# Two stages of a graph kernel joined into one program: feed-forward layer and second attention

## The reference

```python
# layer 0
attn = softmax(q @ k.T / sqrt(32))                       # 8 heads
out  = sum_r (attn * (adj == r)) @ (x @ Wv[r])           # 4 relations
x    = layernorm(x + out @ Wo + bo)
x    = layernorm(x + gelu(x @ W1 + b1) @ W2 + b2)        # feed-forward, width 1024
# layer 1
e    = leaky_relu(q @ k.T, 0.2)                          # 8 heads of 32
attn = softmax(where(adj > 0, e, -9e15))
h    = layernorm(attn @ v)
out  = layernorm(concat(h, x) @ Wffn.T) + x
```

## Time and profile before

| | before |
|---|---|
| median of 3 runs | 3193.49 us (3193.42 to 3193.79) |
| the profiled execution | 3191.47 us |
| its span, first to last instruction | 3189.7 us |
| mean granted clock of PE | 0.98 of full |
| PE busy | 3005.9 us, 94% |
| DVE, ACT, POOL busy | 2509.3, 1999.1, 1683.6 us |
| feed-forward, first to last matmul | 1207.6 to 1881.1 us |
| second attention, from its first load's issue | 1894.3 us to the end |

### The profile page before, as it was taken

How to read it: one execution, slowest core, us unless ns; L and a number is a source line. 1 busy time by engine, 2 the same in 40 slices (tenths; PEclk the granted TensorE clock), 3 DMA queues, 4 the chain that set the end, 5 groups by cost and what they waited for, 6 DMA issues and landing times. The chain is left out here.

```text
span 3189.7 us, 74979 instructions
## 1 busy us (share of the span) xinstructions
PE 3005.9 (94%) x27720; PEld 2053.4 (64%) x27909; DVE 2509.3 (79%) x6757; ACT 1999.1 (63%) x3695; POOL 1683.6 (53%) x1510
## 2 busy tenths in 40 slices
PE   6999999999999958999999977999999999999996
PEld 4666666666666635666666645777777777777774
DVE  5888888888888855776667646888888888888883
ACT  3666666666665635666666634777777777777774
POOL 2555555554555542444444442666666666666665
PEclk9999999999999989999999989999999999999998
DMA  5444444454545413222222213444444444444441
GB/s 158 139 135 137 137 134 142 132 143 133 145 128 144 128 55 101 74 79 75 72 80 79 68 60 121 144 140 142 143 134 135 146 135 142 145 135 135 146 131 44
DMA packets 358328, 382.45 MB, mean 120 GB/s; under 512 B 99265, under 2 KB 266817, under 8 KB 357953
## 3 DMA queue, kind: packets, MB, share of 16 engines
q1 hardware_dynamic: 356800, 376.03, 39.3%
q10 hardware_dynamic: 1152, 1.52, 0.2%
HBM read 242.16 MB, written 118.49 MB: 113 GB/s over the span
## 5 line engine op out<-in xcount | busy, mean ns | idle before, releaser
L2456 DVE TENSOR_TENSOR f_gl<-f_act,f_gh 128x512 f16<-128x512 f32 x256 | 302.9, 1185 | 205.4 <-ACT f_act L2382 205.3
L1844 ACT ACTIVATE b_prob<-b_score_t 128x512 f32<-128x512 f32 x512 | 304.4, 595 | 246.0 <-PE b_score_t L2107 245.9
L2034 DVE CUSTOM_DVE_ANT_0 b_junk<-b_score,b_mask 128x256 bf16<-128x256 f32 x1024 | 390.3, 418 | 40.6 <-issue 40.3
L1408 DVE TENSOR_TENSOR a_linked<-a_prob,a_mask 128x1024 f32<-128x1024 f32 x256 | 356.9, 1395 | 2.3 <-ACT a_prob L1205 2.2
L1928 POOL TENSOR_TENSOR b_half_sum<-b_prob 128x512 f32<-128x512 f32 x256 | 335.5, 1311 | 42.9 <-ACT b_prob L1844 42.6
L2377 ACT ACTIVATE f_gh<-f_up,s_f_b 128x512 f16<-128x512 f32 x256 | 175.5, 686 | 255.1 <-PE f_up L2506 255.0
L1205 ACT ACTIVATE a_prob<-a_score_t 128x1024 f32<-128x1024 f32 x256 | 259.5, 1014 | 110.8 <-PE a_score_t L1488 104.4
L1916 POOL TENSOR_TENSOR b_nw_root<-b_nw_var,b_minus_halves 128x2 f32<-128x2 f32 x128 | 113.1, 883 | 404.9 <-DVE b_nw_neg_mean L1975 404.9
L1401 DVE TENSOR_REDUCE a_neg_max<-a_score 128x4 f32<-128x1024 f32 x256 | 307.2, 1200 | 4.1 <-PE a_score L1501 4.1
L1850 ACT ACTIVATE b_score_t<-b_score_t 128x512 f32<-128x512 f32 x512 | 305.6, 597 | 0.3 <-PE b_score_t L2116 0.3
L2504 PE MATMUL f_down<-s_w,f_gh 128*128 128x256 f16 x1024 | 279.2, 273 | 1.3 <-DVE f_gl L2456 1.3
(11 more groups left out here) (233 smaller groups left out, 9149.5 us busy)
## 6 DMA issues: line engine op xcount, KB each, us to landing
a_stack<-qk_scratch SPq DMA_DIRECT2D x384, 128.0 KB, 3.0
b_stack<-qk_scratch SPq DMA_DIRECT2D x384, 128.0 KB, 2.8
qk_scratch<-a_qk SPq DMA_DIRECT2D x64, 512.0 KB, 2.9
qk_scratch<-b_qk SPq DMA_DIRECT2D x64, 512.0 KB, 2.8
a_x_sb<-x_t SPq DMA_DIRECT2D x64, 256.0 KB, 3.2
a_adj_sb<-adj_t SPq DMA_DIRECT2D x64, 256.0 KB, 3.3
a_res<-x_nodes SPq DMA_DIRECT2D x64, 256.0 KB, 3.4
after_attention<-a_z_out SPq DMA_DIRECT2D x64, 256.0 KB, 2.5
```

The costliest lines, as they stand in the source:

```text
L1408: nc.vector.tensor_tensor(linked[:, k], prob[:, k], mask[:, be[1] % 2].unsqueeze(1).to_broadcast([P, 2, NT * N]), ALU.mult).then_inc(link_ ...
L1844: nc.scalar.activation(prob[:, he], score_t[s][:].rearrange("p t n -> p (t n)"), ACT.Exp, scale=ALPHA).then_inc(exp_done, 1)
L2034: last = nc.vector.tensor_tensor_reduce(junk[:, s, it], score[s][:, it], mask[:, i, it], -1.0, 3e38, ALU.add, ALU.min, neg_max[:, i, col:c ...
L2456: nc.vector.tensor_tensor(gl[:, bu[1] % 2, f], act32[:, f % 2], gh[:, bu[1] % 2, f], ALU.subtract).then_inc(low_done, 1)
```

## The change

`feed_forward` and `attention_second` no longer have blocks of their own. Each returns, for every engine, a function `slot(t, h)` that issues the instructions of one eighth of a step, and a new function calls the two in turn inside one block:

```diff
+def feed_forward_and_second(nc, mid1, mid2, out, adj, adj_t, scr, scr_m, shared, w, late):
+    JOIN = 31
+    CONSTANTS = JOIN - 6
...
+        banks = {k: ctx.enter_context(nc.psum_tensor("bank_" + k, [P, 512], F32)) for k in (
+            "pair0", "pair1", "heads", "sums", "proj", "back", "score0", "score1")}
+        first_rows = ctx.enter_context(nc.sbuf_tensor("first_rows", [P, 2, 2, HQ, DC * N], F16))
...
+        def run(first_slot, second_slot, constants=None):
+            for n in range(JOIN + second["steps"]):
+                for h in range(H):
+                    if n < first["steps"]:
+                        first_slot((n // U, n % U), h)
+                    if constants and n == CONSTANTS and h == 7:
+                        constants(n)
+                    if n >= JOIN:
+                        second_slot(((n - JOIN) // U, (n - JOIN) % U), h)
```

So step `n` of the whole holds step `n` of the feed-forward (up to 34) and step `n - 31` of the attention. The end of the feed-forward's block, the wait for its last store there, the barrier of its block and the start of the attention's block are gone. For both sets of buffers to fit, some are shared and some made smaller:

```diff
-        down = [psum(f"down{i}", [P, 512]) for i in range(4)]
+        row, up, down = banks["proj"], [banks["pair0"], banks["pair1"]], [banks["heads"], banks["sums"]]
...
-        x_sb = sb("x_sb", [P, 4, TT, D], F32)
-        xb = sb("xb", [P, 4, TT, D], F32)
+        x_sb = sb("x_sb", [P, 2, TT, D], F32)
+        xb = sb("xb", [P, XBS, TT, D], F32)
...
-                        if f % 2 == 0 and (n := after(back(bd, 1), TT, k + 1)) is not None:
-                            pe.wait_ge(y_ready, n)
+                        if f % 2 == 0 and number(bd) * TT + k >= 2:
+                            pe.wait_ge(y_ready, number(bd) * TT + k - 1)
...
-    XS = 4
+    XS = 2
...
-        prob = sb("prob", [P, H, NT * N], F32)
-        half_sum = sb("half_sum", [P, H, N], F32)
+        prob = over("gh", 0, [P, H, NT * N], F32)
+        half_sum = over("xb", 0, [P, H, N], F32)
```

```diff
-            nc.gpsimd.memset(stack[KQ:P, :, 1], SHIFT).then_inc(stack_set, 1)
+            def first_constants(n):
+                pool.wait_ge(finished["roots"][0], 2 * (n - 1))
+                wait_old(pool, "row_out", "split")
+                nc.gpsimd.memset(first_rows[KQ:P, :, 1], SHIFT).then_inc(stack_set, 1)
...
+            def late_constants():
+                wait_old(pool, "down_done", "roots")
+                nc.gpsimd.memset(late_rows[KQ:P, :, 1], SHIFT).then_inc(stack_set, 1)
```

More of the change, by code:

```diff
@@ L1597, in attention_first, with attention_second @@
     nc.all_engine_barrier()
[L1600 removed]
+def attention_second(nc, ctx, x_in, x_out, adj, adj_t, scr, scr_m, ident, late, banks, first_rows, old, finished):
     L = "b_"
@@ L1766, in column, with sync, slot @@
             return (h % HQ) * DC * NT + (h // HQ) * NT + it
-        block = ctx.enter_context(nc.Block())
-        @block.sync
-        def _(sp):
+        def sync(sp):
             def held(value):
                 return value if value is None or isinstance(value, int) else sp.to_reg(value)
-            def step(t):
-                for h in range(H):
+            def slot(t, h):
+                if True:
                     if bx := due(t, h, "load"):
@@ L1918, in root, with slot @@
                 nc.gpsimd.tensor_tensor(shift[k][:], s["neg_mean"][:], s["root"][:], ALU.mult).then_inc(root_chain[k], 1)
-            def step(t):
-                for h in range(H):
+            def slot(t, h):
+                if True:
+                    if number(t) == LATE and h == 0:
+                        late_constants()
                     if half := half_due(t, h, "halved"):
@@ L1950, in step, with vector @@
                         nc.gpsimd.tensor_tensor(z_out[:, i], z_out[:, i], res[:, i], ALU.add).then_inc(affine, 1)
-            run_steps(pool, step, STEPS_TAIL)
-        @block.vector
-        def _(dve):
+            return slot, first_constants
+        def vector(dve):
             nc.vector.memset(minus_halves[:], -0.5)
@@ L2081, in step, with tensor @@
                         norm_stats(bg, 1, y[:, bg[1] % 2], y_ready)
-            run_steps(dve, step, STEPS_TAIL)
-        @block.tensor
-        def _(pe):
+            return slot
+        def tensor(pe):
             def three(out, lhs_h, lhs_l, rhs_h, rhs_l, start, stop):
@@ L2243, in step, with feed_forward @@
                         last.then_inc(sums_turned, 1)
-            run_steps(pe, step, STEPS_TAIL)
-    nc.clear_and_free_semaphores(sems)
-    nc.all_engine_barrier()
-def feed_forward(nc, x_in, x_out, shared, w, late):
+            return slot
+        return {"sync": sync, "scalar": scalar, "gpsimd": gpsimd, "vector": vector, "tensor": tensor, "steps": B + STEPS_TAIL}, sems
+def feed_forward(nc, ctx, x_in, x_out, shared, w, late, banks, first_rows):
     G = 2
@@ L2438, in step, with vector @@
                     nc.gpsimd.tensor_tensor(shift[:], s["neg_mean"][:], s["root"][:], ALU.mult).then_inc(root_chain, 1)
-            run(pool, step)
-        @block.vector
-        def _(dve):
+            return slot
+        def vector(dve):
             nc.vector.memset(minus_halves[:], -0.5).then_inc(prep, 1)
@@ L2450, in _, with slot @@
             nc.vector.tensor_scalar(late["far_ident"][:], ident[:], FAR, None, ALU.mult)
-            def step(t):
+            def slot(t, f):
                 bx, bu, bd, bn = stages(t)
-                for f in range(FC):
+                if True:
                     if have(bu):
@@ L2496, in step, with tensor @@
                     nc.vector.tensor_scalar(s["neg_mean"][:], mv[:, :, 0], -1.0, None, ALU.mult).then_inc(seed_chain, 1)
-            run(dve, step)
-        @block.tensor
-        def _(pe):
+            return slot
+        def tensor(pe):
             def three(out, lhs_h, lhs_l, rhs_h, rhs_l, start, stop):
```

279 lines of the change are left out of this document (170 added, 109 removed).

## The result

| | before | the change |
|---|---|---|
| median of 4 runs | 3193.64 us (3193.42 to 3194.10) | 3156.49 us (3153.71 to 3160.38) |
| ratio | | 0.9878, 95% interval 0.9865 to 0.9890 |
| profiled execution, its span | 3191.47 us, 3189.7 us | 3157.04 us, 3155.3 us |

The change is faster by 37.2 us, 1.2%; 3157.0 us were predicted. The runs of the change scatter more than these four of before (6.7 us against 0.7), and in the later measurements the kernel before scatters as much, from 3185.04 to 3198.25 us. So a step of the argument is read from the traces and not from these medians.

What follows compares the result with a forecast made beforehand. From 1881.08 to 1950.53 a chain bounds the kernel, elsewhere PE's own list. Step 4 of the attention starts at 1914.1 instead of 1950.53, 36.4 us less: 3155.0 profiled, 3157 median; range 3150 to 3167.

Steps and rivals of the forecast that it cites:

- Step 32: Feed-forward step 32 with attention step 1: 20.85 us plus 4.7 of PE work and 0.2 for DVE, ending at 1874.6.
- Step 33: Feed-forward step 33 with attention step 2: 11.4 us plus 6.2 of added work and 0.6 of waiting, ending at 1892.8.
- Scores of graph 1: In attention step 3, PE waits 4.3 us for graph 1's rows through the scratch tensor; scores start at 1897.9.
- Rest of step 3: From graph 1's scores to attention step 4: 15.1 us as before, with matmuls at half clock behind the wait.
- Second memset: POOL's 3.5 us memset near DVE's mask: delays the offset 0 or 2.3 us; half, 1.1 us, taken.
- First memset, banks, places: Step 25's memset, two down banks and fewer or moved buffer places in the feed-forward: 0 cost, 1 us kept for the memset's range.
- Barrier and stores: At the join of the stages: their cost vanishes in what is already counted, since PE no longer waits for them.
- weaving rival: Attention held back until the feed-forward ends: only store, barrier and block start saved, some 13 us; 3180 us; chance 0.04.
- waiting links: In steps 32 to 34, some six links each cost 1.5 to 2 us, 10 us come back: 3167 us; chance 0.12.
- slower loop: Late y with two down banks stops PE every feed-forward step; at 1.5 us a step 3203 us; chance 0.08.
- no weaving: Same as the weaving rival: attention waits for the feed-forward's end, some 13 us saved, 3180 us; chance 0.04.
- the one that keeps the clock up: At graph 1's rows PE waits under 2 us and the clock may hold: 3150 to 3152 us; chance 0.14.

Runs made afterwards that it cites:

- e5: The change measured again, unedited, against the kernel before; 3158.62 us, 0.9891 of before, join 136.2 us.
- e9: e7 plus a tiny unused Exp on ACT behind the moved normalisation, so the table load falls in ACT's idle time; 3156.18 us, join 138.1 us.
- e11: The change plus 40 matmuls of 256 columns, unused by the result, on PE ahead of the scores of graph 1; 3155.54 us, join 133.6 us.
- e8: The change with the second memset issued before POOL's last feed-forward root, in slot 7 of step 33; 3154.65 us, join 136.3 us.
- e3: The change with the attention started 4 slots (half a step) earlier; 3167.26 us, join 144.5 us.
- e1: The change with the attention started at step 35, behind the feed-forward, so nothing is woven in; 3187.83 us, join 168.8 us.
- e12: The change with e10's order and 20 of e11's unused matmuls; 3150.98 us, 0.9883 of before, join 129.4 us.
- e4: The change with the attention started 6 slots earlier; 3157.67 us, join 138.6 us.
- e7: The change with the last feed-forward normalisation on ACT and POOL issued in slot 1 instead of slot 3; 3153.34 us, join 136.3 us.
- e2: The change with the attention started two feed-forward steps later, at step 33; 3176.9 us, join 151.4 us.
- e6: The change with the attention started one feed-forward step later; 3166.94 us, join 146.0 us.
- e10: The change with the attention's part of each slot ahead of the feed-forward's in steps 32 and 33; 3155.38 us, join 132.3 us.

## Why the prediction was right

The number came out within 0.5 us, and part of that is luck. The sum forecast 36.4 us for the join, and 35.6 were measured; the profiled execution was to take 3155.0 us and took 3157.04; the medians of two sets of 4 runs lie 37.2 us apart, with a scatter of 6.7 us in one of them. Measured again (e5), the change took 0.9891 of before, some 35 us less, so the 37.2 us are not good to a microsecond. Times of the change are put back by 0.9 us here, the part of the earlier trace rows's shift that is not its own.

- **Step 32**: predicted 25.75 us, measured 26.38. The 4.7 us of PE work were 5.0 (25.76 busy against 20.79). The 0.2 us of waiting were 0.62, for the low part of k (L2028 on DVE). The instruction that was held beside POOL's `z_out` (2.69 us at 1864.74) was not the `f_gl` that I named but one of the attention, ahead of k: `b_qk` in L2109, 2.84 us at 1865.13, where it takes 0.69 at 1903.97.
- **Step 33**: predicted 18.2 us, measured 17.76, with the 0.78 us at its head (0.7 predicted) and 0.39 us for graph 0's rows (0.6 predicted).
- **Scores of graph 1**: predicted wait 4.3 us, measured 4.70; predicted start 1897.9, measured 1898.5. The passage through the scratch tensor took 8.4 us from the store's issue (1889.19), 8.3 were taken from the earlier trace rows. Half clock behind, as forecast, though for 3.0 us and not for 5.7.
- **Rest of step 3**: predicted 15.1 us "as before", measured 16.34. This step failed: it took over one dip of the clock from the kernel before, and there are two. The second costs 1.65 us (6.58 against 4.93 for the same work), and e9 and e11, in each of which it is absent, give it back in this stretch; up to there the change is 0.5 us quicker than before (9.76 against 10.22), its first dip being the shorter one.
- **Second memset**: predicted 1.1 us, between 0 and 2.3; measured 0, for a memset of 3.51 us where half of the earlier trace rows's gave 3.5. The text weighed two starts 0.1 us apart; they were 0.6 apart, `mask` first at 1894.67 and the memset at 1895.28, which is the case for which it said that nothing is lost. It had the slack of the offset as 1.2 us (1896.7 against 1897.9), and 1.4 were measured. The forecast was half of the way between two ends of which only one can happen, so it had to miss by about 1 us. The upper end, 2.3 us, was not put to the test: e8 costs nothing because its memset comes earlier still, and the estimate above for one just ahead of `mask` is 1.9. The lock itself, for which the prediction drew on the Trainium skill, SBUF — State Buffer, section "SBUF: two separate sides", is what e3 and e8 show: the held instruction ends within 0.02 to 0.3 us of POOL's end.
- These two terms, 1.1 too much and 1.2 too little, cancel. Steps 32 and 33 cancel as well, 0.6 us longer and 0.4 shorter. What is left of the 0.8 us is the scores of graph 1, 0.6 us late.
- **First memset, banks, places**: predicted 0, and nothing shows. The up to 3.5 us that the text allowed a DVE difference beside a memset did not come; POOL and DVE of the change in step 25:

```profile
1726.59 3.51 POOL L1938 MEMSET first_rows<- 32x4096 f16 x1
...
1728.09 0.69 DVE L2488 TENSOR_TENSOR f_gl<-f_act,f_gh 128x512 f16<-128x512 f32 x1 [1.91 <-ACT f_act L2416]
```

The same 560 us of the feed-forward, before and then now:

```profile
1240.00:1800.00 560.00, 559.98 (x3861) 377.53 (x3860) 387.35 (x654) 348.78 (x569) 239.04 (x133) 1.00 0.27 75
```

```profile
1240.00:1800.00 560.00, 560.00 (x3868) 378.51 (x3866) 370.36 (x654) 349.18 (x570) 232.92 (x135) 1.00 0.27 75
```

PE is never idle in either. DVE is busy 17 us less, its `f_gl` taking 1.10 us in the mean in place of 1.19, which fits `xb` having left the slots where three were held in a row; PE did not wait for DVE, so nothing comes of it.

- **Barrier and stores**: the weaving rival put what they save at 13 us. e1 has just that, and its join is 2.8 us shorter. That rival's saving was too large by some 10 us.
- **The profiled gain** is 34.4 us, of which the join is 35.6 and the common front 0.9; from the seventh transpose to the end the change is 2.1 us slower (1187.1 against 1185.0). 1.6 of these lie in the last 95 us, where the clock falls at different places in the two; the end, before and then now, from 45.3 us behind the same transpose on:

```profile
3140.00:3170.00 30.00, 19.28 (x184) 11.94 (x186) 9.41 (x38) 17.18 (x34) 19.09 (x22) 1.00 0.11 36
3170.00:3189.70 19.70, 5.73 (x28) 3.91 (x28) 2.62 (x9) 1.93 (x4) 7.55 (x8) 0.59 0.07 27
```

```profile
3104.00:3134.00 30.00, 20.76 (x186) 12.38 (x186) 9.56 (x41) 16.62 (x33) 18.07 (x21) 0.92 0.11 36
3134.00:3155.30 21.30, 6.39 (x28) 4.17 (x28) 2.63 (x9) 2.78 (x5) 8.57 (x9) 0.58 0.06 25
```

No experiment was made on this tail. The rivals of waiting links, of a slower loop and of no weaving are ruled out by the rows above; the one that keeps the clock up did not come true in the change. e11 keeps the clock up with the wait still there, for 2.4 us less join; e12 has the shorter wait as well, which is that rival in full, and its join is 6.7 us shorter, where the rival gave 5 to 7.

## What to carry to other kernels

Where one stage hands over to the next, look first at which chain fills the gap, and only then at the barrier: removing it gave 3 us here, and laying the next stage's latency-bound first steps beside the last stage's matmuls gave over 30. Behind a long wait of TensorE (4.7 us in the change) count the stretch at half clock as a term of its own, and count the waits one by one, since a link that is shortened can hand its idle time, and the clock's fall with it, to the next transfer that is not ready, as in e4 and e9. An overlap moved by a few slots can make two engines meet that held each other off nowhere else, so try more than one offset and read a length between two fixed instructions, which came out at 136.1 and 136.2 us in the two profiles of the change, where whole runs scattered by 5 us or more.

## What the runs showed of the hardware

- Beside POOL's memset, DVE's `BATCH_NORM_STATS2` (0.43 us at 1888.84 in e8) ran at its usual time, and in the change the score maxima, the offset and a difference that reads PSUM (0.68 us at 1896.14) did so too, all inside the memset of 1895.28 to 1898.79. `TENSOR_SCALAR` from SBUF was held until the memset's end, even with 4 elements, and whatever stood behind it on DVE with it. A `TENSOR_TENSOR` with both inputs in SBUF was not held by a memset (`f_gl`, 0.69 us at 1728.09), but it was beside POOL's `z_out`, which reads SBUF (`f_gl` 2.46 us in the earlier trace rows; `b_qk` of L2109 2.84 us for 0.69).
- PE's wait of 1.87 us for a relu in the change was followed by half clock, and so were e7's and e1's of 2.21 us; the same wait of 2.21 us in the kernel before, in e2 and in e6 was not, nor were e9's of 0.79, e12's of 1.33 and e11's of 1.56 us. The length of a wait alone does not tell whether the clock falls; what does stays open.
- Matmuls whose result nobody reads held the clock at 1.00 through a wait of 4.7 us; 2.40 us without work, in e10, were followed by 0.84 and 0.74.
- The table load that the change's trace shows ahead of the first exp costs ACT 1.28 us, once; with it moved into idle time, PE's wait behind it fell from 2.21 us (e7) to 0.79 (e9).
